# Expert blocks: the last output products go inside the branch, the next block's first products between the branches

## The reference

```python
def _L0_ffn_ref(x, Wr, W1, W2):          # N_EXPERTS = 8, TOP_K = 2, CAP_FACTOR = 1.25
    ...
    cap = max(math.ceil(t * TOP_K * CAP_FACTOR / N_EXPERTS), 1)
    y = jnp.zeros_like(xf)
    for e in range(N_EXPERTS):
        ...
        vals, idx = jax.lax.top_k(g_masked, cap)
        g = jnp.where(jnp.isfinite(vals), vals, 0.0)
        xe = xf[idx]
        h = jax.nn.relu(xe @ W1[e]) @ W2[e]
        y = y.at[idx].add(g[:, None] * h)
```

## Time and profile before

| what | us |
|---|---|
| median of three runs (2023.88 to 2026.37) | 2024.39 |
| the profiled execution, its own time | 2027.68 |
| its span, from the first to the last instruction | 2026.0 |
| TensorE busy in the span | 1940.2 |
| VectorE, ScalarE, GpSimd busy | 1000.5, 715.7, 476.6 |

### The profile page before, as it was taken

How to read it: one execution, slowest core, us unless ns; L and a number is a source line. 1 busy time by engine, 2 the same in 40 slices (tenths; PEclk the granted TensorE clock), 3 DMA queues, 4 the chain that set the end, 5 groups by cost and what they waited for, 6 DMA issues and landing times.

```text
span 2026.0 us, 30188 instructions
## 1 busy us (share of the span) xinstructions
PE 1940.2 (96%) x11419; PEld 1722.4 (85%) x11419; DVE 1000.5 (49%) x2471; ACT 715.7 (35%) x1928; POOL 476.6 (24%) x560
## 2 busy tenths in 40 slices
PE   5999999999679999999999999999999999999997
PEld 4888888888468889998898889888988888889896
DVE  5888888887574362243224323522343353236221
ACT  4866667766222151122112211421232142124111
POOL 2555455555311111011101110211101020111101
PEclk9999999999769999999999999999999999999999
DMA  7131223311233162034103400521242143115102
GB/s 213 36 89 55 70 53 89 89 55 54 79 135 93 23 190 47 1 101 129 30 2 94 136 21 13 157 72 32 51 134 62 15 135 94 32 28 160 31 7 26
DMA packets 96316, 148.40 MB, mean 73 GB/s; under 512 B 8608, under 2 KB 50096, under 8 KB 96160
## 3 DMA queue, kind: packets, MB, share of 16 engines
q1 hardware_dynamic: 80288, 109.41, 17.1%
q0 software_dynamic: 15872, 36.71, 10.1%
HBM read 110.70 MB, written 35.39 MB: 72 GB/s over the span
## 4 chain that ended last, share of the span: by engine, by line
PE 70%; DVE 1%; issue 1%; POOL 0%; POOLq 0%; ACT 0%; DVEq 0%
PE psH L1720 34%; PE psY L1720 32%; PE psY L1759 2%; PE psX L1734 2%; PE psI L1782 1%; DVE w_lo L1135 0%; PE psI L1772 0%; POOL out_dram L1504 0%; DVE hT_lo L1694 0%; POOLq L1416 0%; ACT hT_hi L1534 0%; PE psI L1788 0%; DVE moves L1570 0%; DVE onehot L1578 0%; DVE slot_tile L1655 0%
## 5 line engine op out<-in xcount | busy, mean ns | idle before, releaser
L1694 DVE SCALAR_TENSOR_TENSOR hT_lo<-psH,hT_hi 128x384 fp32r<-128x384 f32 (+1 forms) x384 | 209.7, 546 | 869.1 <-ACT hT_hi L1534 529.3
L1534 ACT ACTIVATE hT_hi<-psH 128x384 fp32r<-128x384 f32 (+1 forms) x384 | 185.2, 482 | 1065.1 <-PE psH L1720 1065.1
L1720 PE MATMUL psH<-xgT_hi,w_hi 128*128 128x256 f32 (+3 forms) x1536 | 477.2, 311 | 9.0 <-issue 8.2
L1720 PE MATMUL psH<-xgT_lo,w_hi 128*128 128x256 f32 (+3 forms) x1536 | 475.1, 309 | 3.7 <-issue 3.7
L1720 PE MATMUL psH<-xgT_hi,w_lo 128*128 128x256 f32 (+3 forms) x1536 | 476.2, 310 | 2.1 <-issue 2.1
L1720 PE MATMUL psY<-w_hi,hT_hi 128*128 128x512 f32 (+1 forms) x921 | 371.7, 404 | 1.5 <-DVE hT_lo L1694 1.5
L1720 PE MATMUL psY<-w_lo,hT_hi 128*128 128x512 f32 (+1 forms) x921 | 362.5, 394 | 0.0
L1720 PE MATMUL psY<-w_hi,hT_lo 128*128 128x512 f32 (+1 forms) x921 | 362.3, 393 | 0.0
L1720 PEld LDWEIGHTS psH<-xgT_hi,w_hi 128*128 128x128 f32 x1536 | 291.0, 189 | 37.1 <-issue 20.1
L1720 PEld LDWEIGHTS psH<-xgT_lo,w_hi 128*128 128x128 f32 x1536 | 291.3, 190 | 16.4 <-issue 1.5
L1720 PEld LDWEIGHTS psH<-xgT_hi,w_lo 128*128 128x128 f32 x1536 | 291.0, 189 | 2.6 <-issue 2.6
(11 more groups left out here) (229 smaller groups left out, 2854.1 us busy)
## 6 DMA issues: line engine op xcount, KB each, us to landing
stage<-in_L_ffn_W_dram SPq DMA_DIRECT2D x128, 512.0 KB, 4.6
x_sb<-in_x_dram SPq DMA_DIRECT2D x8, 896.0 KB, 5.6
x_res<-in_x_dram SPq DMA_DIRECT2D x8, 896.0 KB, 5.5
out_dram<-x_res SPq DMA_DIRECT2D x8, 896.0 KB, 4.8
xn_rows<-xn SPq DMA_DIRECT2D x8, 896.0 KB, 4.8
c_sb<-in_ctx_dram SPq DMA_DIRECT2D x8, 384.0 KB, 6.1
c_sb<-in_ctx_dram SPq DMA_DIRECT2D x32, 96.0 KB, 5.7
out_dram<-zrow SPq DMA_DIRECT2D x9, 256.0 KB, 4.4
```

Of the source, the lines that this page charges most:

```text
L1534: h = nc.scalar.activation(hT[0][:, f % 2, 0:m], psH[f % 2][:, 0:m], ACT.Relu)
L1694: h = nc.vector.scalar_tensor_tensor(out=hT[1][:, f % 2, 0:m], in0=psH[f % 2][:, 0:m], scalar=0.0, in1=f32(hT[0][:, f % 2, 0:m]), op0=ALU. ...
L1720: mm = nc.tensor.matmul(out, stationary(a, c), moving(b, c), start=first and c == chunks[0] and j == 0, stop=last and c == chunks[-1] and ...
```

## The change

On TensorE every block's last output product moves into both bodies of the branch, with that body's number of tiles, and becomes the last thing in it. `hidden(n, 0)` moves behind it, out of the bodies, to a place between the end of one branch and the entry of the next. The register load for block n + 1 stands ahead of `hidden(n, 0)`. On VectorE `y_out(n - 1)` moves ahead of block n's first low part.

```diff
             for n in range(NBLOCKS):
                 e, k = divmod(n, NBLK)
+                if n:
+                    y_out(n - 1)
                 for f in range(FCH):
                     m = cols(k)
                     dve.wait_ge(h_hi, FCH * n + f + 1)
...
                     h.then_inc(h_lo, 1)
-                    if f == 0 and n:
-                        y_out(n - 1)
...
                     output(n, f - 1, full)
-                if k == SHARED:
-                    hidden(n + 1, 0, True)
-                    output(n, FCH - 1, full)
+                output(n, FCH - 1, full)
...
-            hidden(0, 0, True)
             full = more(0)
             for n in range(NBLOCKS):
-                if n % NBLK == SHARED:
-                    after = more(n + 1)
-
+                after = more(n + 1) if n + 1 < NBLOCKS else None
+                hidden(n, 0, True)
                 with pe.If(full == 1):
                     steps_from_one(n, True)
                 with pe.Else():
                     steps_from_one(n, False)
-                if n % NBLK == SHARED:
-                    full = after
-                    continue
-                if n + 1 < NBLOCKS:
-                    hidden(n + 1, 0, True)
-                    full = more(n + 1)
-                output(n, FCH - 1, True)
+                full = after
```

## The result

The change made the kernel slower: 2047.31 us as the median of four runs (2041.49 to 2050.54) against 2025.38 for four runs of the kernel before on the same chip (2023.88 to 2028.0), a ratio of 1.0104 with a 95% interval from 1.009 to 1.0117. The forecast was 2019.5. The profiled execution took 2046.0 us, its span 2044.3.

The account below looks back on a forecast made before the run. TensorE, busy 1940.2 of 2026.0 us, was taken as the bound, with stops at branches. Terms summed to -4.45 us, -4.9 with the clock lean, taking 2024.4 to 2019.5; forecast 2017.5 to 2021.5 (53 in 100), wider range 2016.0 to 2023.3.

Parts of the forecast that it names:

- fewer matmuls: On TensorE, nine small blocks each lose the third tile's three output matmuls, 27 x 0.23: -6.2 us.
- last low part: In nine small blocks only output product 14 covers chunk 15's ReLU and low part; it just fits: +0.5 us.
- load before block 0: Two register loads run while TensorE waits for its first input, so the branch begins earlier: -0.35 us.
- entries with no jump just before: Blocks 1, 2, 3, 11, 16, 17, 20 to 23: cover some 3.46 us, 3.3 at first blocks; stops 3.7 to 4.1: +0.4 us.
- exits of full blocks: All 17 queued matmuls become output matmuls, so only the longest branch should still stop TensorE: -1.4 us.
- full block followed by a small one: Entries of 10, 13, 15, 19: only a load and twelve matmuls between jumps, 2.0 us of cover: +4.4 us.
- second stops: Landings shortly before a multiple of 256 instructions, entries of 1, 11, 19 and exit of 14: 7.9 to 6.1 us, -1.8.
- clock: Half clock behind block 19's stops: no change taken, bounds 1.7 us both ways, leaning half a microsecond to a gain.
- cover 3.5 becomes 4.1 us: At full blocks' exits, queued work hiding the branch grows because all 17 matmuls ahead are now output matmuls.
- The sequencer's own waits took 51 ns each: Waits at the head of `hidden`, all 79 at 51 ns; cited against the sequencer being held ahead of `hidden(n, 0)`.
- third rival: Sequencer held ahead of `hidden(n, 0)`, cover 2.1 instead of 3.4 us at eleven entries: +14 us, 2034; 6 in 100.
- `y_out` first: On VectorE, its 2.07 us of products run beside `hidden(n, 0)`: no cost; without that cover up to 2 us a block.

Follow-up runs that it names:

- Experiment 1: Changed kernel with chunk 15's W1 product ahead of chunk 13's output product, its ReLU and low part in separate memory: 2032.24 us, ratio 1.0013.
- experiment 2: Changed kernel with all 24 flag registers loaded once before the first expert block, no load between branches: 2047.66 us, ratio 1.0089.
- experiment 11: Changed kernel with chunk 15's W1 product early, code shifted by tiny matmuls, and each register load behind `hidden(n, 0)`: 2021.79 us, ratio 0.9966.
- 8: Kernel before with chunk 15's W1 product early, all flags loaded early, and 44 tiny matmuls shifting the code: 2017.35 us, ratio 0.9945.
- experiment 12: Kernel before with chunk 15's W1 product early and 57 tiny matmuls shifting the code, flags loaded at their old places: 2017.22 us, ratio 0.9946.
- experiment 9: Changed kernel with its code shifted by 50 tiny matmuls ahead of the experts: 2040.38 us, ratio 1.0055.
- experiment 3: Changed kernel with `y_out` back at its old place, behind chunk 0's low part on VectorE: 2047.33 us, ratio 1.0094.
- experiment 6: Kernel before with only VectorE's part of the change, `y_out` of the block before ahead of the first low part: 2045.79 us, ratio 1.0085.
- 5: Kernel before with its code shifted by 47 tiny matmuls ahead of the experts' first product: 2019.3 us, ratio 0.995.
- 4: Changed kernel with chunk 15's W1 product early and all flag registers loaded first: 2036.85 us, ratio 1.0044.
- experiment 7: Kernel before with every block in the old middle-block form, next first product and chunk 15's output ending both bodies, 27 matmuls fewer: 2039.78 us, ratio 1.0052.
- 10: Changed kernel with chunk 15's W1 product early and its code shifted by 50 tiny matmuls: 2021.5 us, ratio 0.9963.

## Why the prediction was wrong

| step | forecast | measured |
|---|---|---|
| fewer matmuls | -6.2 | -6.2 (27 fewer, at the price of before) |
| last low part | +0.5 | +1.5 (1.7 less 0.2 in the waits) |
| load before block 0 | -0.35 | +0.2 (1.41 to 1.65) |
| entries with no jump just before | +0.4 | +2.4 (3.7 to 6.1) |
| exits of full blocks | -1.4 | +11.5 (2.1 to 13.6) |
| full block followed by a small one | +4.4 | +4.3 (3.85 to 8.15) |
| second stops | -1.8 | +2.1 (7.9 to 10.0) |
| clock | -0.5 | about +4.5 |

The measured column adds up to 20.3; the span grew by 18.3, and the experts began 1.9 us earlier in that execution (first product at 578.03 instead of 579.91), which makes 20.2. Two sums of the forecast were off by little: the four second stops make 6.2, not 6.1, and with only block 8's exit still stopping, for some 0.5 us, the exits would have gained 1.6, not 1.4.

- **The step that failed: "cover 3.5 becomes 4.1 us".** It rests on "15 to 17 matmuls are ahead", counted in the old order and carried over to the new one as 17 output matmuls, as if TensorE's sequencer were always that far ahead. It is that far only where nothing ahead of the branch waits. With chunk 15's output product right ahead of the branch, its wait for the low part decides: cover 2.50 us at block 4 and 2.75 at block 5 (934.88 + 0.23 - 932.36). The step "The last low part" saw that wait, but asked only whether TensorE would run dry, not what the branch behind it does meanwhile. Experiment 1 let that wait be met earlier, with the same matmuls, and 15 us came back. (The 13.6 us of the table count block 14's exit with 1.45, from a restart 0.55 us behind the jump's end.)
- **The same step left out the load.** Behind the landing of a jump that has outlasted its cover nothing is queued, so a load there delays the next matmul: 0.60 us at block 4. By the rows of experiment 2 (0.17 instead of 0.52 to 0.60 us at the exits) it is about 3 of the 11.5 us. What the time would gain without it in the changed kernel stays open, since that experiment also started later and moved the landings. Once the exits are covered the load is hidden: experiment 11 moved it with no effect, and 8 against 12 says the same.
- **"The sequencer's own waits took 51 ns each"** was used against the third rival. It was no evidence: in the changed kernel too all 78 have 51 ns. The Trainium skill ("Perfetto Trace Analysis", Sequencer-only Instruction (DRAIN, etc)) says why: the profiler reports only the execution, not the wait in front of it. The trace agrees, with no spread in 78 rows. The slower rival named the right mechanism at the wrong wait, the one ahead of `hidden(n, 0)`; the entries kept 3.0 us of cover (632.14 to 635.17 at block 1), not 2.1.
- **Entries.** In first and middle blocks the cover was 2.9 and 3.05 us, not 3.3 and 3.46: their first product stands behind both the wait for the last low part and the load, and is queued later than assumed (3.2 to 3.4 us without the load, in experiment 2, and 3.3 to 3.4 with the wait met early, in experiment 1). In third blocks it was 3.44, as assumed. The ten branches took as long together as before (37.7 us), so the stops grew by 2.4 us instead of 0.4.
- **The entries behind an exit** were right in kind, and their sum in size (8.15 us against 8.3), the latter in part by luck: the stops were 2.3, 2.1, 1.6 and 2.1 us, not 1.8, 1.8, 2.7 and 2.0, and the one at block 15 was the shortest only because the branch there began 5.3 us behind the landing, after the long stop (3.75 in experiment 9, without it). The places of the four second stops were right too. Their sizes were not: 4.7 us (5.25 less the usual 0.55) instead of 2.3 at block 14, 2.0 instead of 1.5 at block 1 and 1.5 instead of 0.6 at block 19.
- **The clock** was put at no change; the stops at blocks 10, 15 and 19 brought 20.4 us at half. Of these, the stretch at 1532 hid partly behind the branch of block 15; what the others and its second half cost is half of the time in which TensorE streamed, 1.9 + 2.6 + 1.7 us, less 1.7 before.
- **`y_out` first** costs nothing that can be told here, as forecast (experiment 3), for the reason given: 17 us without that cover (experiment 6).

What stays open: why one branch takes 3.2 and another 4.1 us at the same distance from others, why experiment 9's came out longer at blocks 11, 15 and 17, and why block 15's entry took up to 6.6 us.

## What to carry to other kernels

The cover of a jump is what is queued when the last wait ahead of it is met (here up to 17 matmuls), not a fixed number of instructions: put work between the instruction that waits and the branch, or make what it waits for early. Count the stops, the removed work and the clock of each stretch as separate sums; 6.2 us of removed matmuls stayed invisible behind 21 us of new stops. Where code jumps, look at where it lands: 47 tiny matmuls that only move the code gave 0.5% (2019.3 us). The fastest kernel found here (experiment 12, 2017.2 us) has such a shift too, and what its reordering adds to it is within the noise.

## What the runs showed of the hardware

- A branch begins about 0.1 us after the wait of the instructions ahead of it is met (862.00 to 862.10, 932.27 to 932.36), although eighteen instructions of the output product lie between. The Trainium skill ("Perfetto Trace Analysis", Tensor Engine Instruction (MATMUL, LD_WEIGHTS)) lets the sequencer decode on while a matmul waits for its semaphore; that would allow the 0.1 us, but the branch itself did not pass the waiting ones at any of the nine exits.
- A branch that starts shortly behind another's landing is longer: at the entry of block 10 it took 3.58 to 4.18 us when it began 1.1 to 1.4 us behind (before, experiments 5, 6, 8 and 12), and 4.33 to 4.84 at 0.2 to 0.7 (after, experiments 1 to 4, 7 and 9 to 11). Both ranges say one thing: from the landing of block 9's exit to the end of block 10's branch it is 4.7 to 5.3 us in all fourteen kernels, wherever in that time the branch begins. At blocks 13 and 19 it is 4.75 to 5.4 us wherever the branch begins within 1.6 us; at block 15 it is 5.0 to 7.2. So what decides the stop there is how much work is queued between that landing and the second branch (21 matmuls before, 12 after, none in experiment 7, for stops of 0.5, 2.3 and 5.2 us at block 10), and not how far behind the landing the branch begins.
- A landing with up to 30 instructions left before a multiple of 256 stops the engine a second time, by up to 5.0 us (block 14's exit with one left, experiments 1 and 3), unless the next branch jumps away ahead of that multiple: the exit of 18 had 27 left in experiments 2 and 4, and no second stop. With 36 to 43 left it depends: behind a full block's exit the next branch came 2.3 us late (38, 39 and 43 left); at small blocks' entries TensorE lost 0.3 us or less in most cases (36, 37, 39, 40 and 42 left), but 1.9 us at block 3 of experiment 7 (40 left).
